# Convolution by three products in place of four from the third double on, both of a double in a row, y carried to its partitions by DMA

## The chip, the cores and the metric

The kernel runs on one core of a Trainium2 chip. The metric is the device time of one execution, in microseconds, and lower is better. The kernel before takes 180.75 us (median of three runs, 180.70 to 180.76).

## The reference, cut to what matters

```
N, C_IN, L = (32, 64, 1024)
C_OUT, K, GROUPS = (64, 9, 4)
out = lax.conv_general_dilated(x, weight, window_strides=(1,), padding=[(4, 4)],
                               dimension_numbers=('NCH', 'OIH', 'NCH'), feature_group_count=GROUPS)
ctx = jnp.einsum('nd,od->no', c, c_weight)
y = out + ctx[:, :, None] + bias[None, :, None]
w = kernel.astype(x.dtype) * 2.0 - 1.0          # 1024 x 1024, signs
x = x + scale * jnp.einsum('bsi,if->bsf', y, w)
```

So each of 32 images (64 channels, 1024 positions) goes through a grouped convolution of nine taps, gets a shift for each channel, and its positions are multiplied by a 1024x1024 matrix of signs; the result, scaled, is added to x. All is float32.

## The kernel before, in words

Two images are a row (128 partitions of x: `2 d + r` is the row, 16 rows), and two rows, r = 0 and 1, are a double d of 0 to 7. `M` = 128, `B` = 8: a position is 8 m + u, and m becomes the partition of y.

**Convolution.** For a row, `to_phases` (L358, ScalarE) splits x into its 8 phases, `x_phase`. SP then issues eight transfers (`to_blocks`, `to_block`, L195) that gather 16 channels x 8 phases into the 128 partitions of a block `x_blk[r][:, a]`; a is one of two images times four groups. `conv` (L650, matmuls at L658) multiplies, for each of the eight blocks, two shifted views of 128 columns (`s` = 0 and 1) with two Toeplitz matrices of the taps, and adds both in PSUM: 16 matmuls a row. `add_shift` (L475, VectorE) adds the shift and writes `y_sum[r]`.

**Products.** y of a double is cut into A11, A12 (row 0) and A21, A22 (row 1). From double 1 on the multiplication by the signs is done in Winograd's form, seven products P1 to P7 in place of eight, with the sums S1 to S4 (`combine`, L492) as operands. Each operand is split in a high part (`high_part`, ScalarE, L373, a cast to fp32r) and a low part (`low_part`, VectorE, L502, the difference), and a product is four matmuls of 512 columns with each (L681). `sum_up` (L513, VectorE) adds a product from its PSUM bank A, B or C to x in `x_nat`; the names of the sums, C11_P2 to C21_A, give the quarter of the output and the bank or product. Double 0 is done with eight plain products (`PLAIN`, L698).

**Order.** Each engine takes its work in the order that is written out in its `step(d)`; semaphores tie the engines together. TensorE in step d: P2, P1, convolution of row 0 of double d + 1, P6, P5, convolution of row 1, P7, P3, P4. ScalarE: the high parts of S3, S4 and A22 of d, the phases of row 0 of d + 2, high parts of A12 and A11 of d + 1, phases of row 1, high parts of S1 and S2 of d + 1. VectorE: the sums as the products end, with the low parts, shifts and combinations between them. SP: the block transfers of both rows of d + 2, the loads of x of d + 3, the stores of d. GpSimd has work in the first 21 us only. `runs(d, 2)` is true where there is a double d + 1, `runs(d, 4)` where there is a d + 2.

## Time and profile before

| what | value |
| --- | --- |
| median of three runs | 180.75 us (180.70 to 180.76) |
| the profiled execution, its own time | 180.59 us |
| its span, first to last instruction | 178.8 us |
| mean granted clock of TensorE | 0.99 |
| TensorE, weight loads, VectorE, ScalarE, GpSimd busy | 171.2, 147.5, 127.5, 68.1, 7.4 us |
| instructions | 2874 |
| DMA | 27.35 MB, 153 GB/s over the span |

Busy is the time in which an engine had an instruction running. The chain of waits follows the work that ended last back to what released it, so it tells which engine sets the time. In the profile an fp32 matmul or weight load is two records. The issue of a transfer is an instruction of its queue; "to landing" is the time from the issue to the last byte.

### The profile page before, as it was taken

To read this page: it belongs to the slowest core of one execution; us is meant where nothing else is said; L and a number is where in the kernel's file an instruction comes from. 1 tells how busy PE (TensorE), PEld (TensorE's weight loads), DVE (VectorE), ACT (ScalarE), POOL (GpSimd) and SP (SyncE) were. 2 spreads that over 40 slices of the span, in tenths; PEclk is the share of its full clock that TensorE was granted. 3 is DMA by queue.
4 is the path that set the end of the run, shared out by engine and by line. 5 is a ranking of instruction groups with operands and counts; after the bars stand their busy time and mean duration, and the time that the engine had idled before them with its cause. 6 is when DMAs were issued, how large, how long until landed. Compare 5 with 4: busy or idle time off the path is not lost.

```text
span 178.8 us, 2874 instructions
## 1 busy us (share of the span) xinstructions
PE 171.2 (96%) x1010; PEld 147.5 (83%) x1010; DVE 127.5 (71%) x188; ACT 68.1 (38%) x77; POOL 7.4 (4%) x18
## 2 busy tenths in 40 slices
PE   7699999999999999999999999999999999998991
PEld 2379888898989889988989898988998898986781
DVE  5736466979996877687675967596766877587662
ACT  3203993566452543329071634237061502042000
POOL 4230600000000000000000000000000000000000
PEclk9969999999999999999999999999999999999999
DMA  5589697768886792776757793778463650005006
GB/s 216 132 152 279 206 262 188 186 105 207 192 283 164 104 343 47 109 167 125 283 84 175 116 318 56 130 146 204 192 96 55 90 233 0 2 0 235 4 0 235
DMA packets 23629, 27.35 MB, mean 153 GB/s; under 512 B 2752, under 2 KB 19072, under 8 KB 23616
## 3 DMA queue, kind: packets, MB, share of 16 engines
q1 hardware_dynamic: 22176, 25.63, 56.8%
q0 software_dynamic: 368, 1.07, 2.4%
q10 hardware_dynamic: 1072, 0.48, 1.3%
q8 instruction: 8, 0.13, 0.3%
q14 instruction: 5, 0.04, 0.1%
HBM read 10.32 MB, written 8.40 MB: 105 GB/s over the span
## 4 chain that ended last, share of the span: by engine, by line
PE 93%; DMA 2%; DVE 1%; ACTq 1%; issue 0%; DVEq 0%
PE ps_conv L658 33%; PE ps_A L681 28%; PE ps_C L681 14%; PE ps_B L681 7%; DMA taps_nat<-weight 2%; PE ps_B L698 2%; PE ps_A L698 2%; PE ps_toep L698 2%; PE ps_C L698 2%; PE ps_toep L681 1%; PE ps_toep L636 1%; PE ps_C L647 1%; DVE sums L214 1%; PE ps_A L624 1%; DVE x_nat L513 0%
## 5 line engine op out<-in xcount | busy, mean ns | idle before, releaser
L658 PEld LDWEIGHTS ps_conv<-toeplitz,x_blk 128*128 128x128 f32 x512 | 60.4, 194 | 2.6 <-issue 0.8
L658 PE MATMUL ps_conv<-toeplitz,x_blk 128*128 128x128 f32 x512 | 60.8, 278 | 0.0
L475 DVE TENSOR_TENSOR y_sum<-ps_conv,shift 128x512 f32<-128x512 f32 (+1 forms) x33 | 22.2, 674 | 17.4 <-PE ps_conv L658 12.4
L373 ACT CAST hi_S<-sums 128x512 fp32r<-128x512 f32 x28 | 16.6, 620 | 43.4 <-DVE sums L492 42.7
L373 ACT CAST hi_A<-y_sum 128x512 fp32r<-128x512 f32 x24 | 14.0, 616 | 41.5 <-DVE y_sum L475 41.5
L358 ACT COPY x_phase<-x_nat 128x1032 f32<-128x1032 f32 x13 | 28.3, 2177 | 3.0 <-DMA x_nat<-x 3.0
L513 DVE SCALAR_TENSOR_TENSOR x_nat<-ps_A,scale_col,x_nat 128x512 f32<-128x512 f32 x27 | 20.3, 750 | 11.2 <-PE ps_A L681 11.2
L502 DVE TENSOR_TENSOR lo_S<-sums,hi_S 128x512 fp32r<-128x512 f32 x28 | 19.0, 680 | 0.0
L502 DVE TENSOR_TENSOR lo_A<-y_sum,hi_A 128x512 fp32r<-128x512 f32 x24 | 16.3, 682 | 1.7 <-ACT hi_A L373 1.7
L681 PE MATMUL ps_A<-sign_T,hi_S 128*128 128x512 f32 x56 | 16.2, 412 | 1.1 <-DVE x_nat L513 0.9
L681 PE MATMUL ps_A<-sign_T,lo_S 128*128 128x512 f32 x56 | 15.0, 389 | 0.0
L513 DVE SCALAR_TENSOR_TENSOR x_nat<-ps_C,scale_col,x_nat 128x512 f32<-128x512 f32 x14 | 10.5, 747 | 3.8 <-PE ps_C L681 3.8
L681 PEld LDWEIGHTS ps_A<-sign_T,lo_S 128*128 128x128 f32 x56 | 10.5, 188 | 2.3
L681 PEld LDWEIGHTS ps_A<-sign_T,hi_S 128*128 128x128 f32 x56 | 9.6, 189 | 2.9 <-issue 1.6
L492 DVE TENSOR_TENSOR sums<-y_sum 128x512 f32<-128x512 f32 x14 | 9.5, 686 | 0.3
L681 PE MATMUL ps_C<-sign_T,hi_S 128*128 128x512 f32 x28 | 7.5, 390 | 0.0
L681 PE MATMUL ps_B<-sign_B,hi_A 128*128 128x512 f32 x28 | 7.5, 389 | 0.0
L681 PE MATMUL ps_B<-sign_B,lo_A 128*128 128x512 f32 x28 | 7.5, 389 | 0.0
L681 PE MATMUL ps_A<-sign_B,hi_A 128*128 128x512 f32 x28 | 7.5, 389 | 0.0
L681 PE MATMUL ps_C<-sign_T,lo_S 128*128 128x512 f32 x28 | 7.5, 389 | 0.0
L681 PE MATMUL ps_C<-sign_B,hi_S 128*128 128x512 f32 x28 | 7.5, 389 | 0.0
L681 PE MATMUL ps_C<-sign_B,lo_S 128*128 128x512 f32 x28 | 7.5, 389 | 0.0
(104 smaller groups left out, 174.3 us busy)
## 6 DMA issues: line engine op xcount, KB each, us to landing
x_nat<-x SPq DMA_DIRECT2D x16, 512.0 KB, 4.2
out<-x_nat SPq DMA_DIRECT2D x15, 512.0 KB, 4.8
x_blk<-x_phase SPq DMA_DIRECT2D x118, 64.5 KB, 2.5
w_bytes<-w_bool SPq DMA_DIRECT2D x2, 512.0 KB, 6.3
shift<-shift_dram POOLq DMA_DIRECT2D x1, 768.0 KB, 6.1
x_blk<-x_phase ACTq DMA_DIRECT2D x6, 64.5 KB, 3.7
x_blk<-x_phase POOLq DMA_DIRECT2D x4, 64.5 KB, 3.0
out<-x_nat SPq DMA_DIRECT2D x1, 256.0 KB, 2.9
```

Source lines behind the costliest of these rows:

```text
L214: return copy(skewed, taps_nat[:, :, :].rearrange("o c k -> o k c").unsqueeze(1) .to_broadcast([C, hi_ - lo_, TAPS, CG]))
L358: nc.scalar.copy(x_phase[r][:, :, 0:M + 1], line(d, r, 0, PAD + L + PAD).rearrange("r (m q) -> r q m", q=B)).then_inc(phase_ok[r], B)
L373: nc.scalar.copy(hi[k][:, :, :], flat(operand(k))).then_inc(hi_ok[k], 1)
L475: nc.vector.tensor_tensor(y_sum[r][:, u, a, :].rearrange("m u a o -> m a u o"), ps_conv[:, a, u, :], shift_of(d, r, a).unsqueeze(2).to_bro ...
L492: nc.vector.tensor_tensor(flat(operand(k)), flat(operand(left)), flat(operand(right)), op).then_inc(s_ok[k], 1)
L502: nc.vector.tensor_tensor(lo[k][:, :, :], flat(operand(k)), hi[k][:, :, :].bitcast(F32), ALU.subtract).then_inc(lo_ok[k], 1)
L513: nc.vector.scalar_tensor_tensor(there, bank[b], scale2_col[:, :], there, ALU.mult, ALU.add).then_inc(summed[k], 1)
L624: nc.tensor.matmul(bank["A"], warm[:, 0:P], warm[:, :], start=True, stop=True)
L636: now = nc.tensor.transpose(ps_toep[:, s, u], taps_exp[:, B * s + u].rearrange("o c q -> o (c q)"), ident[:, :])
L658: now = nc.tensor.matmul(ps_conv[:, a].rearrange("m u o -> m (u o)"), x_blk[r][:, a, s:s + M], toeplitz[:, s, g].rearrange("r u o -> r u ( ...
L681: now = nc.tensor.matmul(dest, part[of][:, u, :], signs[SIGNS_OF[k]][:, KH - 1 - u, c:c + dest.shape[-1]], start=start and u == 0 and part ...
L698: now = nc.tensor.matmul(bank[b], part[of][:, u, :], signs[k][:, KH - 1 - u, :], start=opens and u == 0 and part is hi, stop=not opens and ...
```

## The change

From double 2 on the convolution of a row is made of three products. K = 64: the phase-split positions m are taken as even and odd. Where the four products were even and odd columns with the Toeplitz matrices 0 and 1, now the odd columns are multiplied with the sum of both matrices (`toeplitz[:, 2]`), and the differences of neighbouring columns with one matrix each; the shifted first product is added to the second for even positions, and the third is subtracted for odd ones. A group's two images share a matmul (2 x 64 columns), so there are 3 x 4 matmuls a row.

- GpSimd makes the differences (`differences`), ScalarE copies the odd columns (`odd_blocks`), each for every row.
- VectorE's `fast_y` takes three operations a row and writes `y_two`, whose partitions hold image and half position; ScalarE issues four transfers a row (`to_parity`) that carry it to `y_sum` with the partitions as before.
- Both convolutions stand one after the other, between P1 and P6, and share three PSUM banks.
- Casts and low parts of A11 and A12, of S1 and S2, and of S3 and S4 are made in one instruction each of twice the size (`SPLITS`).
- VectorE makes S3 and S4 after C21_A of the step before; the low part of S12 comes behind C11_P1, that of A behind C22_A.
- On ScalarE the order is S34, odd columns of row 1, A22, both phase copies, the transfers of y, odd columns of row 0 of d + 2, A, S12.
- `x_nat` has 12 slots in place of 16, so the last loads wait for the first stores; each store has a semaphore. The shift is loaded by image in two transfers.

The diff, cut to its core:

```diff
-OPERANDS = "A11", "A12", "A22", "S1", "S2", "S3", "S4"
+OPERANDS = "A11", "A12", "S1", "S2", "S3", "S4", "A22"
+SPLITS = {"A": ("A11", "A12"), "S12": ("S1", "S2"), "S34": ("S3", "S4"), "A22": ("A22",)}
+SPLIT_OF = {k: of for of, ks in SPLITS.items() for k in ks}
...
         x_phase = [sb(f"x_phase{s}", [P, B, PITCH]) for s in range(2)]
-        x_blk = [sb(f"x_blk{s}", [P, NG, PITCH]) for s in range(2)]
-        y_sum = [sb(f"y_sum{r}", [P, B, NG, CG]) for r in range(2)]
-        sums = sb("sums", [P, 4, KH, NG, CG])
+        x_blk = [sb(f"x_blk{s}", [P, NG, BLK_PITCH]) for s in range(2)]
+        y_two = [sb(f"y_two{r}", [P, 2, B, C]) for r in range(2)]
+        y_sum = [sb(f"y_sum{r}", [P, 2, B, C]) for r in range(2)]
+        sums = sb("sums", [P, 4, KH, 2, C])
...
...
+        ps_small = ps_conv[:, 2].rearrange("d g u o -> d (g u o)")
         ps_cond = ps_small[:, 0:N]
         ps_cw = ps_small[:, N:N + C]
...
+        def order(d, r):
+            return 2 * (d - 2) + r
+        def line(d, r, lo_, hi_):
+            return x_nat[:, (2 * d + r) % SLOTS, lo_:hi_]
...
         def to_block(eng, r, a, landed):
-            eng.dma_start(x_blk[r][:, a, 0:M + 1], x_phase[r][a * CG:(a + 1) * CG, :, 0:M + 1]
+            i, g = a // GROUPS, a % GROUPS
+            eng.dma_start(x_blk[r][:, 2 * g + i, 0:M + 1], x_phase[r][a * CG:(a + 1) * CG, :, 0:M + 1]
                           ).then_inc(landed, 16)
...
+        def group(k):
+            if k == "A":
+                return y_sum[0][:, :, :, :].rearrange("m i u c -> m u i c")
+            if k in ("S12", "S34"):
+                n = 0 if k == "S12" else 2
+                return sums[:, n:n + 2].rearrange("m n u i c -> m (n u i c)")
+            return operand(k)
...
         def _(sp):
             def load(d, r, landed):
+                if 2 * d + r >= SLOTS:
+                    sp.wait_ge(stored[2 * d + r - SLOTS], 16)
                 sp.dma_start(line(d, r, PAD, PAD + L), row(x_pairs, d, r)).then_inc(landed, 16)
             def to_blocks(d, r):
-                sp.wait_ge(conv_done[r], 2 * d)
+                if d < 3:
+                    sp.wait_ge(conv_done[r], 2 * d)
+                else:
+                    sp.wait_ge(dif_ok[r], 2 * (d - 2))
+                    sp.wait_ge(odd_ok[r], d - 2)
                 sp.wait_ge(phase_ok[r], B * (d + 1))
                 for a in range(NG):
...
                                   x_nat[:, 2, :].rearrange("r (m q) -> r q m", q=B)).then_inc(phase_ok[0], B)
             pool.wait_ge(shift_out, 16)
-            shift_flat = shift[:, :, :, :].rearrange("p j a o -> p (j a o)")
-            rest = slice(EARLY * C, N * C)
-            pool.dma_start(shift_flat[:, rest], shift_dram[:, rest].to_broadcast([P, N * C - EARLY * C])
-                           ).then_inc(shift_in, 16)
+            for i in range(2):
+                pool.dma_start(shift[i * K:(i + 1) * K].rearrange("p j o -> p (j o)"),
+                               shift_by_image[i:i + 1].rearrange("i j o -> i (j o)").to_broadcast([K, PAIRS * C])
+                               ).then_inc(shift_in, 16)
+            def differences(d, r):
+                if d > 2:
+                    pool.wait_ge(m_done[0], order(d - 1, r) + 1)
+                    pool.wait_ge(m_done[2], order(d - 1, r) + 1)
...
+                for h in range(2):
+                    wait_blocks(pool, d, r, h)
+                for e in range(2):
+                    nc.gpsimd.tensor_tensor(dif[r][:, e], x_blk[r][:, :, e:e + M:2], x_blk[r][:, :, e + 1:e + 1 + M:2][:, :, 0:K],
+                                            ALU.subtract).then_inc(dif_ok[r], 1)
+            for d in range(2, DOUBLES):
+                for r in range(2):
+                    differences(d, r)
...
+            def odd_blocks(d, r):
+                if d > 2:
+                    act.wait_ge(m_done[1], order(d - 1, r) + 1)
+                elif r == 1:
+                    for k in ("B11", "B12", "B21", "B22", "T3"):
+                        act.wait_ge(sign_ok[k], KH)
+                for h in range(2):
+                    wait_blocks(act, d, r, h)
+                nc.scalar.copy(odd[r], x_blk[r][:, :, 1:1 + M:2]).then_inc(odd_ok[r], 1)
+            def to_parity(d, r):
+                act.wait_ge(lo_ok["A" if r == 0 else "A22"], d - 1)
+                for k in (("S2", "S3", "S4") if r == 0 else ("S1", "S3")):
+                    act.wait_ge(s_ok[k], d - 1)
+                for p, made in ((0, y_even_ok), (1, y_odd_ok)):
+                    act.wait_ge(made, order(d, r) + 1)
+                    for i in range(2):
+                        act.dma_start(y_sum[r][p::2, i], y_two[r][i * K:(i + 1) * K, p]).then_inc(y_in[r], 16)
...
             def step(d):
-                for k in ("S3", "S4", "A22"):
-                    high_part(k, d)
+                high_part("S34", d)
+                if runs(d, 2):
+                    odd_blocks(d + 1, 1)
+                high_part("A22", d)
                 if runs(d, 4):
                     to_phases(d + 2, 0)
-                if runs(d, 2):
-                    high_part("A12", d + 1)
-                    high_part("A11", d + 1)
-                if runs(d, 4):
                     to_phases(d + 2, 1)
                 if runs(d, 2):
-                    high_part("S1", d + 1)
-                    high_part("S2", d + 1)
+                    to_parity(d + 1, 0)
+                    to_parity(d + 1, 1)
+                if runs(d, 4):
+                    odd_blocks(d + 2, 0)
+                if runs(d, 2):
+                    high_part("A", d + 1)
+                    high_part("S12", d + 1)
...
+            def fast_y(d, r):
+                n = order(d, r)
+                even, uneven = (y_two[r][:, p].rearrange("m u (g o) -> m g u o", g=GROUPS) for p in range(2))
+                dve.wait_ge(m_done[1], n + 1)
+                dve.wait_ge(shift_in, 32)
+                if d > 2:
+                    dve.wait_ge(y_in[r], 16 * 4 * (d - 2))
+                nc.vector.tensor_tensor(uneven, ps_conv[:, 1],
+                                        shift[:, 2 * d + r].rearrange("m (g o) -> m g o", g=GROUPS).unsqueeze(2)
+                                        .to_broadcast([P, GROUPS, B, CG]), ALU.add).then_inc(mid_ok, 1)
+                dve.wait_ge(mid_ok, n + 1)
+                dve.wait_ge(m_done[0], n + 1)
+                nc.vector.tensor_tensor(even, ps_conv[:, 0], uneven, ALU.add).then_inc(y_even_ok, 1)
+                dve.wait_ge(m_done[2], n + 1)
+                nc.vector.tensor_tensor(uneven, uneven, ps_conv[:, 2], ALU.subtract).then_inc(y_odd_ok, 1)
...
             def step(d):
                 if d > 1:
                     sum_up("C21_A", d - 1)
-                    low_part("S2", d)
+                    combine("S3", d)
+                    combine("S4", d)
                 sum_up("C11_P2", d)
-                low_part("S1", d)
                 sum_up("C11_P1", d)
-                low_part("S3", d)
+                if d > 1:
+                    low_part("S12", d)
                 if runs(d, 2):
-                    add_shift(d + 1, 0, 0)
-                low_part("S4", d)
+                    fast_y(d + 1, 0)
+                low_part("A22", d)
                 if runs(d, 2):
-                    add_shift(d + 1, 0, 1)
-                low_part("A22", d)
+                    fast_y(d + 1, 1)
                 sum_up("C12_A", d)
-                if runs(d, 2):
-                    low_part("A12", d + 1)
+                low_part("S34", d)
                 sum_up("C22_C", d)
-                if runs(d, 2):
-                    low_part("A11", d + 1)
-                    add_shift(d + 1, 1, 0)
-                    add_shift(d + 1, 1, 1)
-                    combine("S1", d + 1)
                 sum_up("C22_A", d)
-                if runs(d, 2):
-                    combine("S3", d + 1)
                 if last(d):
                     finish_last(d)
                 else:
+                    low_part("A", d + 1)
+                    combine("S1", d + 1)
+                    sum_up("C12_C", d)
                     combine("S2", d + 1)
-                    sum_up("C12_C", d)
-                    combine("S4", d + 1)
             first_double()
             for d in range(1, DOUBLES):
...
+            def fast_conv(d, r):
+                n = order(d, r)
+                if n == 0:
+                    pe.wait_ge(y_ok, 16)
+                    pe.wait_ge(both_ok, 1)
+                for m, taps, read in ((1, 2, mid_ok), (0, 0, y_even_ok), (2, 1, y_odd_ok)):
+                    if n:
+                        pe.wait_ge(read, n)
+                    if m == 1:
+                        pe.wait_ge(odd_ok[r], d - 1)
+                    else:
+                        pe.wait_ge(dif_ok[r], 2 * (d - 2) + (1 if m == 0 else 2))
+                    for g in range(GROUPS):
+                        both = slice(2 * g, 2 * g + 2)
+                        of = odd[r][:, both] if m == 1 else dif[r][:, m // 2, both]
+                        now = nc.tensor.matmul(ps_conv[:, m, g].rearrange("m u o -> m (u o)"),
+                                               of.rearrange("r b k -> r (b k)"),
+                                               toeplitz[:, taps, g].rearrange("r u o -> r (u o)"), start=True, stop=True)
+                    now.then_inc(m_done[m], 1)
...
@@ -706,11 +847,10 @@
                 product("P2", d, bank["B"], True, True, "C11_P2")
                 product("P1", d, bank["A"], True, False, "C21_A")
                 if runs(d, 2):
-                    conv(d + 1, 0)
+                    fast_conv(d + 1, 0)
+                    fast_conv(d + 1, 1)
                 product("P6", d, bank["A"], False, False, "C11_P1", 1)
                 product("P5", d, bank["C"], True, False, "C12_C")
-                if runs(d, 2):
-                    conv(d + 1, 1)
                 product("P7", d, bank["A"], False, False, "C12_A", 1)
                 product("P3", d, bank["C"], False, True, "C22_C", 1)
                 if last(d):
```

## Rows read from the trace of the kernel before

**Rows 1.** The page: busy time of the engines; the chain's shares by engine

```profile
PE 171.2 (96%) x1010; PEld 147.5 (83%) x1010; DVE 127.5 (71%) x188; ACT 68.1 (38%) x77; POOL 7.4 (4%) x18
...
PE 93%; DMA 2%; DVE 1%; ACTq 1%; issue 0%; DVEq 0%
```

**Rows 2.** The chain of waits in order of time: start us, us, what

```profile
41.59 1.81 PE ps_B L681 x8
...
65.48 3.57 PE ps_conv L658 x32
...
85.35 3.57 PE ps_conv L658 x32
...
161.19 1.81 PE ps_B L681 x8
...
164.85 0.76 DVE x_nat L513
...
165.75 2.08 PE ps_A L681 x8
```

**Rows 3.** Two steps: busy PE, PEld, DVE, ACT, POOL, granted clock, DMA share, GB/s

```profile
45.20:65.50 20.30, 20.17 (x123) 17.77 (x122) 17.12 (x26) 9.82 (x10) 0.00 (x0) 1.00 0.83 208
65.50:85.35 19.85, 19.85 (x122) 17.64 (x122) 14.60 (x22) 8.24 (x9) 0.00 (x0) 1.00 0.63 135
```

**Rows 4.** Groups by line: the convolution's weight loads; busy us, mean ns

```profile
L658 PEld LDWEIGHTS ps_conv<-toeplitz,x_blk 128*128 128x128 f32 x512 | 60.4, 194 | 2.6 <-issue 0.8 <-DVE toeplitz L219 0.5 <-DMA x_blk<-x_phase 0.4
```

**Rows 5.** Groups by line: VectorE

```profile
L475 DVE TENSOR_TENSOR y_sum<-ps_conv,shift 128x512 f32<-128x512 f32 (+1 forms) x33 | 22.2, 674 | 17.4 <-PE ps_conv L658 12.4 <-issue 4.8
...
L502 DVE TENSOR_TENSOR lo_S<-sums,hi_S 128x512 fp32r<-128x512 f32 x28 | 19.0, 680 | 0.0
...
L447 DVE TENSOR_TENSOR sign_T<-sign_B,sign_T 128x1024 fp32r<-128x1024 f32 x4 | 4.8, 1214 | 0.0
```

**Rows 6.** Groups by line: ScalarE

```profile
L358 ACT COPY x_phase<-x_nat 128x1032 f32<-128x1032 f32 x13 | 28.3, 2177 | 3.0 <-DMA x_nat<-x 3.0
...
L373 ACT CAST hi_S<-sums 128x512 fp32r<-128x512 f32 x28 | 16.6, 620 | 43.4 <-DVE sums L492 42.7
...
L347 ACT ACTIVATE sign_T<-w_bytes 128x2048 fp32r<-128x2048 uint8 x1 | 1.9, 1914 | 0.0
```

**Rows 7.** Instructions in order of time, 85 to 106 us: start us, us, engine

```profile
85.39 0.75 DVE L513 SCALAR_TENSOR_TENSOR x_nat<-ps_A,scale_col,x_nat 128x512 f32<-128x512 f32 x1 [0.47 <-PE ps_A L681]
86.05 0.68 DVE L502 TENSOR_TENSOR lo_S<-sums,hi_S 128x512 fp32r<-128x512 f32 x1
...
88.95 5.05 SPq L195 DMA_DIRECT2D x_blk<-x_phase  x8
...
89.75 1.14 ACT L373 CAST hi_A<-y_sum 128x512 fp32r<-128x512 f32 x2 [5.12 <-DVE y_sum L475]
```

**Rows 8.** Instructions in order of time, 0 to 12 us: block transfers issued

```profile
5.09 5.91 SPq L195 DMA_DIRECT2D x_blk<-x_phase  x6
5.10 2.62 ACTq L195 DMA_DIRECT2D x_blk<-x_phase  x3
...
8.78 2.25 ACTq L195 DMA_DIRECT2D x_blk<-x_phase  x3
```

**Rows 9.** DMA issues: KB each, median us from issue to landing

```profile
x_blk<-x_phase SPq DMA_DIRECT2D x118, 64.5 KB, 2.5
...
out<-x_nat SPq DMA_DIRECT2D x2, 128.0 KB, 2.8
```

**Rows 10.** Instructions in order of time, 12 to 46 us: GpSimd, VectorE, block transfers

```profile
18.45 2.19 POOL L316 COPY x_phase<-x_nat 128x1032 f32<-128x1032 f32 x1 [7.86 <-DMA x_nat<-x]
...
19.53 0.69 DVE L475 TENSOR_TENSOR y_sum<-ps_conv,shift 128x512 f32<-128x512 f32 x1 [1.11 <-PE ps_conv L658]
...
28.32 0.69 DVE L502 TENSOR_TENSOR lo_S<-y_sum,hi_S 128x512 fp32r<-128x512 f32 x1 [3.24 <-ACT hi_S L373]
...
40.11 5.05 SPq L195 DMA_DIRECT2D x_blk<-x_phase  x8
```

222 lines of the change are left out of this document (126 added, 96 removed).

## The prediction

> **What bounds the kernel now.** I read the busy shares first: TensorE 96% of the span, VectorE 71%, ScalarE 38%, GpSimd 4% [rows 1]; in each step the granted clock is 1.00, the upper of its two levels [rows 3]. The chain of waits says the same in order of time: TensorE's work follows on TensorE's work, product by product, 93% of the chain [rows 1, 2]. One step of the pipeline is 19.87 us: seven products of 1.81 us (12.7 us) and two convolutions of 3.57 us (65.48 to 85.35) [rows 2]. In that period VectorE is busy 14.6 us, ScalarE 8.2 us and the DMA engines have a share of 0.6 to 0.8 [rows 3]. The longest gap of TensorE after 50 us is in the last step, where P6 waits for the sum of P1, which ends at 165.61 (P6 starts at 165.75, P1 ended 0.02 before that sum began) [rows 2]. So a shorter convolution is worth its full length, until another engine or a loop of several engines needs more than TensorE does in a step. The question is where that point lies.
>
> **What goes from TensorE.** A convolution of a row is 16 matmuls, 32 records (the trace counts each fp32 matmul twice), in 3.57 us, 0.223 us each [rows 2]. The fast form is 12 matmuls of the same shape, 128x128 weights and 128 moving columns, so 2.68 us. That holds if the weight loads stay hidden: they are as many as the matmuls and 194 ns against a record's pitch of 112 ns looks too long, but the same rows run at that pitch now, overlapped [rows 4]. Without that cover a matmul would cost its two loads, 0.39 us, as the upper bound; 0.223 is the price of the same shapes. Saved: 4 x 0.223 = 0.89 us a row, 1.79 a double; double 2 to 7 have 12 rows, so 10.7 us. TensorE alone would have a step of 18.08 us and the run would come to 180.59 - 10.7 = 169.9 us.
>
> **VectorE in a step.** Removed: four additions of the shift (L475, 0.67 us on the mean, 0.69 for a full one). Added: six operations of 512 elements from PSUM (fast_y), at the price of that same row. The seven low parts become three of 1024 elements and one of 512: 1.21 us for 1024 (L447, f32) against 0.68 for 512 [rows 5], so 4.3 us in place of 4.8. Sums (7 x 0.75 [rows 7]) and combinations (4 x 0.68) stay. Total 4.1 + 4.3 + 5.3 + 2.7 = 16.4 us of records; records overlap by some 0.07 us (one of 0.75 is followed 0.66 later by the next [rows 7]; I take 0.60 for one of 0.68), so about 15 us of 18.08. VectorE isn't the bound by itself. The toeplitz sum, once, 0.7 us, lies in the 3.24 us for which VectorE waits at 28.3 us [rows 10] and costs nothing; if that cover went it would cost 0.7. The low part of S12 moves behind the sum of P1: in the last step it ends 1.2 us after that sum while P6 asks for it 0.9 us after: 0 to 0.3 us.
>
> **ScalarE in a step.** Casts: 0.62 us for 512 elements, the pair at 1.14 [rows 7], so a 1024 one at 1.05 (below: 0.62 plus 512 more at the pace of the 2048-element sign in 1.91 us; above: two single ones, 1.24) [rows 6]. Three and one small: 3.8 us. Two copies of odd columns, 512 elements with a stride: between a cast's 0.62 and half a strided 1032-element copy, 1.09 [rows 6]; I take 0.65, since the stride is 8 bytes and not 32. Two phase copies 2 x 2.18. Eight DMA issues of y at 0.6 to 0.75 [rows 8]: 5 to 6 us. Together some 14.5 us of 18: hidden by size, but not by order, which is the point of the next part.
>
> **The loop that the change closes.** ScalarE takes its work in the order written: hi S34, odd blocks of row 1, hi A22, the two phase copies, the y transfers, then the odd blocks of row 0 of the double after next, and only then hi A of the next double. Those odd blocks need all eight block transfers of a row whose phases were made in this same step. Before, nothing on ScalarE waited for them. And hi S34 waits for S4, which VectorE now makes behind low A, S1, C12_C, S2, C21_A and S3. So, from the end of one S4 to the end of the next:
> hi S34 1.05, odd copy 0.65, hi A22 0.62, phase copy 2.18: 4.5. Eight block issues on SP, the last begins 5.05 - 0.6 = 4.45 after the first, and lands 2.5 later [rows 7, 9]: 6.95. Odd copy 0.65, hi A 1.05: 1.7. On VectorE low A 1.21, S1 0.60, C12_C 0.66, S2 0.60, C21_A 0.66, S3 0.60, S4 0.68: 5.0. Six links between engines at 0.04 (between 0.02 and 0.14 [rows 2]): 0.25. Sum 18.4 us, already above TensorE's 18.08. TensorE feels it where P1 of the next double waits for C21_A, four VectorE operations behind low A, and a stall there holds the whole step.
> To that comes what the y transfers do to the block transfers: they are issued in the same 5 us, by ScalarE while SP issues its eight. Where two and three queues issued at once, at 5 to 11 us, SP took 5.91 us for six (0.98 each) and ScalarE 2.25 for three (0.75) in place of 0.63 [rows 8]; and the y transfers bring 8 x 128 KB more into engines that are 0.6 to 0.8 busy. Their own landing, 2.5 (64.5 KB) to 2.8 us (128 KB) [rows 9], is no term: the last is issued some 10 to 12 us into the step, due at 15.8. Bounds for the slowing of the blocks: nothing (18.4), and 0.35 for each of eight issues (21.2). I take 0.08 each, near the lower end since for most of the time only two queues issue and y's have half the descriptors: **19.1 us a step**.
> The first step has SP's four stores and three loads, DMA share 0.83 [rows 3], and the blocks of row 1 land at 45.2 + 2.0 (issued from 40.11 to 45.16, the last 2.5 after its issue began [rows 9, 10]), after which GpSimd makes two differences before the convolution's second and third part: 0.4 to 0.6 us late, in the same 19.1. The pass after it, which first closes the loop behind those transfers, I put 0.9 higher. Six steps: 6 x 19.1 + 0.9 = 115.5 us, where now 41.59 to 161.19 is 119.6 [rows 2]. The gain is 4.1 us: 180.59 - 4.1 = 176.5, and as the profiled execution is 0.16 under the median of 180.75, **176.6 us**. The other changes are hidden: the store semaphores and 12 slots (the loads of doubles 6 and 7 wait for stores issued in the first step, three steps before), the split shift load, cast and low part of A made as one in the first double (due only at 41.59 [rows 2]); each would cost under 1 us once.
>
> **GpSimd.** It is idle from 21 us on and now gets four differences a step, each of two inputs and 512 elements. Price: the only copy of it is 1032 elements in 2.19 us [rows 10], 2.1 ns an element; so 1.1 us if two inputs cost no more than one, 2.2 if they are read one after the other. Four are 4.4 to 8.8 of 18 us. They are due nearly a step later: hidden, as work. In this trace no VectorE operation with two SBUF inputs runs beside GpSimd: at 19.53 an addition from PSUM took its usual 0.69 within GpSimd's copy [rows 10]; so the price of their meeting lies between nothing (no reason speaks for a gain) and a full stop of one for the length of the other's operation; I take nothing, which is what the one meeting in the rows shows, and keep the other end as the first rival.
> The Trainium skill speaks against the change here: "SBUF — State Buffer", section Who interferes with whom, says that a VectorE instruction with two SBUF inputs and a GpSimd one that reads SBUF exclude each other for their whole length, and that one SBUF input doesn't contend. The 0.69 us addition agrees with the second half; no run here yet shows the first. By it the sum would be the first rival's.
>
> **Rivals.**
> *GpSimd holds VectorE up (slower).* The differences of row 0 start when the blocks land, the same moment as the odd copy; VectorE wants low A 1.7 us later and the two differences last 2.2 to 4.4: a wait of 0.5 to 2.7. Those of row 1 begin some 5 us later, when VectorE makes S3 and S4: half to a whole difference, 0.55 to 2.2. Both lie in the loop. At the low price it is 1.05 a step, 20.15; six make 6.3, so 176.6 + 6.3 - 0.4 (the first pair meets nothing) = 182.5; with differences of 2.2 us it is up to 2.2 + 1.65 more in each step. It turns to slower than before from 0.7 us a step. Against it: VectorE may go first, GpSimd has slack. Low parts and combinations are 7 of VectorE's 16 us, so they do meet.
> *The transfers crowd each other.* y and block packets overlap, and the landing goes from 2.5 to 3.5 us or each issue from 0.63 to 0.8: 18.4 + 1.0 to 1.4 = 19.4 to 19.8 a step, 178.4 to 180.8 (6 x 0.3 to 0.7 above the forecast).
> *TensorE stays the bound.* If the odd copy, the links or the casts are cheaper by 0.4, the loop is below 18.1 and the run 170 to 172. Against it: the sum of 18.4 already has the cheap prices.
> *It doesn't do what it says:* 12 matmuls without accumulation that take as long as 16 would leave 19.87 and add stalls, 181 to 183. The weight loads at the same pitch speak against it.
>
> **How the numbers follow.** Loop near 19.1: 0.41, 173.5 to 179. GpSimd's hold: 0.33, of which 0.07 still under 180.4 (short differences), the rest 181 to 188. Crowded transfers: 0.15, of which 0.07 I count as faster, since the two slowings may add. TensorE the bound: 0.08. The last: 0.03. A measurement of this kernel can tell 0.2%, 0.4 us. Faster 0.41 + 0.07 + 0.07 + 0.08 = 0.63, same 0.05, slower 0.32. The range leaves out TensorE as the bound and the upper part of GpSimd's hold: 173.3 to 184.8; that of the likeliest case alone is 173.5 to 179.
>
> **What the profile of the changed kernel would show.** Convolution rows at 0.223 us a matmul, 144 in place of 192 from double 2 on, and TensorE's other groups as they are; a gap ahead of P1 in each step, released by VectorE (C21_A), of 0.7 to 1.2 us; ScalarE's odd copy released by the block transfers, hi A right behind it; block issues on SP of over 0.63 us while ScalarE issues. Wrong if the gap lies ahead of the convolution's second row (VectorE too slow with fast_y), if low A or S3 on VectorE starts at the end of a GpSimd operation or takes far over 1.2 and 0.68 us (the first rival), or if no gap is there at all.

## The result, and the profile of the changed kernel

The changed kernel takes **190.13 us** (median of four runs, 187.15 to 191.82) where the kernel before takes 180.72 us beside it (180.66 to 180.76): a ratio of **1.042, interval 1.031 to 1.052**. It is slower. The forecast was 176.6 us and the range ended at 184.8. Here and below, a ratio leaves out the executions that took over 1.5% more than the fastest of their kernel (here 190.91 and 191.82 us). The profiled execution took 189.35 us, its span is 187.5 us.

The page of the changed kernel: busy time of the engines, then TensorE's row and the granted clock in 40 slices of 4.69 us.

```profile
PE 168.9 (90%) x914; PEld 140.9 (75%) x914; DVE 139.2 (74%) x180; ACT 71.4 (38%) x68; POOL 37.6 (20%) x43
...
PE   7599999999569999998889969998899978999892
...
PEclk9859999999957999999999999999999999999999
```

TensorE has 96 records less but was 96% of the span and is 90% [rows 1]. There is a hole in the 11th and 12th slice, with a lower clock in the 12th and 13th, and a smaller hole in nearly every step from the third on.

The table goes from the start of P2 to the start of the next P2 on TensorE, by its instructions. ([rows 2] has these starts 0.16 us later, since the chain counts a piece from the end of the one before.) Doubles 1 to 7 give six steps.

| | start to first P2 | 1 | 2 | 3 | 4 | 5 | 6 | last P2 to the end |
| --- | --- | --- | --- | --- | --- | --- | --- | --- |
| before | 41.43 | 20.26 | 19.87 | 19.87 | 19.87 | 19.87 | 19.87 | 17.8 |
| forecast | as before | 19.1 | 20.0 | 19.1 | 19.1 | 19.1 | 19.1 | as before |
| after | 42.95 | 25.05 | 18.55 | 20.85 | 21.01 | 20.17 | 20.72 | 18.2 |

The six steps are 126.35 us where before they were 119.6 (+6.75). With 1.5 us before and 0.4 us behind them that is the 8.7 us by which the span grew. Against the forecast (115.5) they are 10.85 us too long: 5.95 in the first step, 6.35 in the last four, and the second is 1.5 short.

The waits of the changed kernel: who waited for what, us in total, times, the longest.

```profile
ACT set L452 <- DMA x_blk<-x_phase: 27.8, 4, 7.4
...
DVE lo L631 <- ACT hi L483: 7.8, 4, 2.3
...
PE ps_A L822 <- DVE x_nat L642: 6.1, 5, 1.4
...
PE ps_conv L803 <- DVE y_two L595: 5.4, 4, 3.5
```

TensorE waits in two places: ahead of P1 for C21_A (in steps 3 to 6, 1.04 to 1.41 us; the fifth wait is the one in the last step that [rows 2] shows too), which was foretold, and ahead of the second row of the convolution for VectorE's first operation of `fast_y` (3.54 us in the first step, 0.43 to 0.80 in three others), which wasn't. The first line is the loop: ScalarE stands up to 7.4 us at its odd copy for the block transfers. (Odd columns and differences lie in the tile `set_0` for row 0 and in the space of `w_bytes` for row 1, which is why the profile calls them `set` and `w_bytes`.)

**One turn of the loop.** Instructions of the changed kernel in order of time, 84 to 113 us: start us, us, engine, line.

```profile
84.12 2.06 POOL L399 TENSOR_TENSOR set<-x_blk 128x512 f32<-128x512 f32 x2 [14.81 <-DMA x_blk<-x_phase]
...
85.71 1.55 DVE L631 TENSOR_TENSOR lo<-y_sum,hi 128x1024 fp32r<-128x1024 f32 x1 [1.93 <-ACT hi L483]
...
88.70 2.78 POOL L399 TENSOR_TENSOR w_bytes<-x_blk 128x512 f32<-128x512 f32 x2 [2.52 <-DMA x_blk<-x_phase]
...
89.93 1.16 PE L822 MATMUL ps_A<-sign_B,hi 128*128 128x512 f32 x4 [1.35 <-DVE x_nat L642]
90.50 1.54 DVE L621 TENSOR_TENSOR sums<-y_sum,sums 128x512 f32<-128x512 f32 x1
...
94.15 2.09 ACT L440 COPY x_phase<-x_nat 128x1032 f32<-128x1032 f32 x1
...
96.33 6.37 SPq L231 DMA_DIRECT2D x_blk<-x_phase  x8
...
96.62 5.70 ACTq L462 DMA_DIRECT2D y_sum<-y_two  x7
...
105.26 0.67 ACT L452 COPY set<-x_blk 128x512 f32<-128x512 f32 x1 [7.00 <-DMA x_blk<-x_phase]
...
105.83 1.05 ACT L483 CAST hi<-y_sum 128x1024 fp32r<-128x1024 f32 x1
...
106.91 1.55 DVE L631 TENSOR_TENSOR lo<-y_sum,hi 128x1024 fp32r<-128x1024 f32 x1 [2.26 <-ACT hi L483]
```

S4 ends at 92.04; the next one begins at 111.51 and takes 1.52, so the turn is 20.99 us. By the terms of the prediction:

| from S4's end | forecast | after |
| --- | --- | --- |
| hi S34, odd copy, hi A22, phase copy (to 96.24) | 4.5 | 4.20 |
| blocks issued and landed (to 105.26) | 6.95 + 0.64 | 9.02 |
| odd copy, hi A (to 106.91) | 1.7 | 1.65 |
| low A to S4 (to 113.03) | 5.0 | 6.12 |
| links | 0.25 | in the rows above |
| a turn | 19.05 | 20.99 |

The chain of work is the foretold one, link for link; two of its terms are too small.

**The first step.** The same view, 46 to 59 us, and under it the busy time in three stretches (PE, PEld, DVE, ACT, POOL, clock, DMA share, GB/s).

```profile
46.76 2.92 PE L803 MATMUL ps_conv<-toeplitz,set 128*128 128x128 f32 x24
47.85 3.20 DVE L559 TENSOR_TENSOR sign_T<-sign_B,sign_T 128x1024 fp32r<-128x1024 f32 x2
...
48.55 3.40 POOL L399 TENSOR_TENSOR w_bytes<-x_blk 128x512 f32<-128x512 f32 x2 [4.17 <-DMA x_blk<-x_phase]
...
50.97 0.74 DVE L642 SCALAR_TENSOR_TENSOR x_nat<-ps_B,scale_col,x_nat 128x512 f32<-128x512 f32 x1
...
52.48 0.68 DVE L595 TENSOR_TENSOR y_two<-ps_conv,shift 128x512 f32<-128x512 f32 x1
...
53.22 5.49 PE L803 MATMUL ps_conv<-toeplitz,w_bytes 128*128 128x128 f32 x24 [3.54 <-DVE y_two L595]
```

```profile
41.00:66.00 25.00, 21.46 (x107) 18.54 (x106) 19.82 (x23) 9.34 (x9) 7.96 (x6) 0.86 0.85 212
86.00:107.00 21.00, 19.02 (x107) 15.97 (x106) 16.39 (x22) 8.81 (x8) 4.65 (x5) 1.00 0.68 194
51.90:58.80 6.90, 5.58 (x25) 5.59 (x26) 4.59 (x8) 1.76 (x1) 0.05 (x1) 0.51 0.78 185
```

VectorE has the two halves of the sign sums for T4 ahead of C11_P2, C11_P1 and `fast_y`. They start at 47.85 and, beside GpSimd's differences, take 3.20 us where two took 2.4 alone [rows 5]. `fast_y` empties the first bank at 53.16, and only then may the second row start: TensorE has stood for 3.54 us. In that gap the granted clock falls to its lower level, 1.2 GHz (0.51 on the mean from 51.9 to 58.8), and the 24 records take 5.49 us in place of the first row's 2.92.

Rows of the page of the changed kernel: two groups by line (busy us, mean ns) and two kinds of DMA issues (KB each, median us to landing).

```profile
L399 POOL TENSOR_TENSOR set<-x_blk 128x512 f32<-128x512 f32 x12 | 12.8, 1088 | 79.2 <-DMA x_blk<-x_phase 79.2
...
x_blk<-x_phase SPq DMA_DIRECT2D x118, 64.5 KB, 3.2
...
y_sum<-y_two ACTq DMA_DIRECT2D x48, 128.0 KB, 3.3
```

### The profile page after: what moved, and what is told of

It is laid out like the page before. It is cut to its first block and busy times, and to the rows that moved or that the text cites. A ratio compares the mean times of both kernels' runs of the same rounds, so it can differ in the third digit from the quotient of the medians.

```text
span 187.5 us, 2763 instructions
## 1 busy us (share of the span) xinstructions
PE 168.9 (90%) x914; PEld 140.9 (75%) x914; DVE 139.2 (74%) x180; ACT 71.4 (38%) x68; POOL 37.6 (20%) x43
## 5 line engine op out<-in xcount | busy, mean ns | idle before, releaser
L483 ACT CAST hi<-sums 128x1024 fp32r<-128x1024 f32 x14 | 14.7, 1049 | 38.9 <-DVE sums L621 19.8
L399 POOL TENSOR_TENSOR set<-x_blk 128x512 f32<-128x512 f32 x12 | 12.8, 1088 | 79.2 <-DMA x_blk<-x_phase 79.2
L803 PE MATMUL ps_conv<-toeplitz,w_bytes 128*128 128x128 f32 x144 | 20.2, 304 | 5.4 <-DVE y_two L595 5.4
L803 PEld LDWEIGHTS ps_conv<-toeplitz,w_bytes 128*128 128x128 f32 x144 | 19.0, 215 | 6.3 <-DVE y_two L595 6.1
L822 PE MATMUL ps_A<-sign_T,hi 128*128 128x512 f32 x80 | 22.7, 405 | 0.9 <-DVE x_nat L642 0.9
L822 PE MATMUL ps_A<-sign_T,lo 128*128 128x512 f32 x80 | 22.0, 396 | 0.0
L399 POOL TENSOR_TENSOR w_bytes<-x_blk 128x512 f32<-128x512 f32 x12 | 16.8, 1422 | 22.3 <-DMA x_blk<-x_phase 22.3
L803 PEld LDWEIGHTS ps_conv<-toeplitz,set 128*128 128x128 f32 x144 | 16.9, 192 | 0.8 <-issue 0.3
L780 PEld LDWEIGHTS ps_conv<-toeplitz,x_blk 128*128 128x128 f32 x128 | 16.5, 209 | 1.3 <-issue 0.8
L631 DVE TENSOR_TENSOR lo<-sums,hi 128x1024 fp32r<-128x1024 f32 x14 | 17.3, 1238 | 0.0
L803 PE MATMUL ps_conv<-toeplitz,set 128*128 128x128 f32 x144 | 17.1, 275 | 0.0
L780 PE MATMUL ps_conv<-toeplitz,x_blk 128*128 128x128 f32 x128 | 16.7, 294 | 0.0
```

The lines of the kernel that those rows point to most:

```text
L399: nc.gpsimd.tensor_tensor(dif[r][:, e], x_blk[r][:, :, e:e + M:2], x_blk[r][:, :, e + 1:e + 1 + M:2][:, :, 0:K], ALU.subtract).then_inc(di ...
L483: nc.scalar.copy(parts(hi_all, k), group(k)).then_inc(hi_ok[k], 1)
L631: nc.vector.tensor_tensor(parts(lo_all, k), group(k), parts(hi_all, k).bitcast(F32), ALU.subtract).then_inc(lo_ok[k], 1)
L780: now = nc.tensor.matmul(ps_conv[:, i, g].rearrange("m u o -> m (u o)"), x_blk[r][:, 2 * g + i, s:s + M], toeplitz[:, s, g].rearrange("r u ...
L803: now = nc.tensor.matmul(ps_conv[:, m, g].rearrange("m u o -> m (u o)"), of.rearrange("r b k -> r (b k)"), toeplitz[:, taps, g].rearrange( ...
L822: now = nc.tensor.matmul(dest, part[of][:, u, :], signs[SIGNS_OF[k]][:, KH - 1 - u, c:c + dest.shape[-1]], start=start and u == 0 and part ...
```

## The experiments

All ratios are to the kernel before, run beside them on the same chip.

### The loop and the first step: the change again, each of two cures alone, and both

The changed kernel once more, as the partner of the others:

> The changed kernel again, unchanged: the yardstick of this set. It took 187.15 to 191.82 us, and in its profiled execution a step from the third on was 20.2 to 21.0 us, the first 25.05. If the late clock fall in the first step (two stretches at the lower level, about 2.8 us) comes in some executions only, this run should again spread over 2 us and more. A product took 1.86 us there and 1.81 in the kernel before: if that lies in the kernel, it is 1.86 here too; if in the execution, some run shows 1.81.

Measured: 191.85 us, 1.062 (1.057 to 1.067). The steps are 24.39, 19.54, 21.38, 21.45, 21.96 and 21.22; the gap ahead of the second row is 4.12 us in the first step and 0.6 to 1.2 in the others, and the clock falls again. The first P2 starts at 41.72, not at 42.95. The seven executions of this kernel lie between 187.15 and 192.67 us, but the two places are the same.

**ScalarE makes hi A before the odd copy.** This cuts the block transfers out of the loop: hi A then needs only y.

```diff
-                if runs(d, 4):
-                    odd_blocks(d + 2, 0)
                 if runs(d, 2):
                     high_part("A", d + 1)
+                if runs(d, 4):
+                    odd_blocks(d + 2, 0)
+                if runs(d, 2):
                     high_part("S12", d + 1)
```

> ScalarE's copy of the odd columns of row 0 of the double after next is put behind the cast of A, nothing else. Theory of the closed loop (cast, copies, block transfers, copy, cast, low part, four VectorE operations, S3, S4): the cast of A no longer waits for the block transfers, the gap of 1.0 to 1.4 us ahead of P1 goes, and steps 2 to 5 fall from 20.2-21.0 to about 19.2: 6 to 7 us in all, 181 to 183. Rival, VectorE is the bound because GpSimd holds it up: the cast comes earlier but low A, S3 and S4 end as late; under 2 us. Rival, transfers: the y transfers land no earlier than the blocks, the cast of A now waits for them: 2 to 4 us.

Measured: 183.10 us, 1.011 (1.006 to 1.016). Steps 25.03, 18.54, then 19.05, 18.99, 18.89, 18.86. The wait ahead of P1 is gone from the third step on. Instructions of this kernel in order of time, 100 to 104 us:

```profile
100.04 1.05 ACT L483 CAST hi<-y_sum 128x1024 fp32r<-128x1024 f32 x1 [4.24 <-DMA y_sum<-y_two]
...
102.60 1.22 DVE L632 TENSOR_TENSOR lo<-y_sum,hi 128x1024 fp32r<-128x1024 f32 x1
...
103.11 0.67 ACT L452 COPY set<-x_blk 128x512 f32<-128x512 f32 x1 [2.02 <-DMA x_blk<-x_phase]
```

hi A is released by y now, 3 us before the blocks of this row have landed. The gaps ahead of the second row go as well, but for the one in the first step. So the closed loop through the block transfers is the cause of some 1.7 us in each of the last four steps (20.69 to 18.95 on the mean; 2.5 us against the 21.50 of the changed kernel's second execution); the first step doesn't move.

**The sign sums for T4 behind `fast_y`.** The call in the first double becomes a function, called for the low half after `fast_y(2, 0)` and for the high half after `fast_y(2, 1)`.

```diff
-                for u in (LOW, HIGH):
-                    sign_sums("T4", plain("B21", u), ALU.subtract, plain("T2", u), u)
...
                     fast_y(d + 1, 0)
+                if d == 1:
+                    sign_t4(slice(0, KH // 2))
                 low_part("A22", d)
                 if runs(d, 2):
                     fast_y(d + 1, 1)
+                if d == 1:
+                    sign_t4(slice(KH // 2, KH))
```

> In the first step VectorE's two sums for the signs T4 (3.2 us) are put behind the three operations on row 0 of the convolution and behind those on row 1, nothing else. In the profile of the changed kernel TensorE stood 3.54 us ahead of the second row of double 2 for the first of these operations, and the granted clock then fell to the lower level for 6.8 us, in which the row took 5.5 in place of 2.7 us. Theory: the gap of the first step shrinks to under 1 us, the clock stays at the upper level, the step falls from 25.05 to about 19: 187.5 - 6 = 181 to 182. Rival, the differences of row 1 on GpSimd come late anyway (they ended at 51.95): the gap shrinks by 1 us only and the clock still falls.

Measured: 188.49 us, 1.039 (1.032 to 1.046). The first step is 19.88 in place of 25.05; the others are no shorter (21.29, 21.02, 21.59, 20.00, 20.83), so the run gains less than the 6 us that were expected. The same place as above in this kernel:

```profile
48.16 2.05 POOL L399 TENSOR_TENSOR w_bytes<-x_blk 128x512 f32<-128x512 f32 x2 [4.11 <-DMA x_blk<-x_phase]
...
49.76 2.94 PE L808 MATMUL ps_conv<-toeplitz,w_bytes 128*128 128x128 f32 x24 [0.41 <-DVE y_two L595]
...
50.94 1.22 DVE L559 TENSOR_TENSOR sign_T<-sign_B,sign_T 128x1024 fp32r<-128x1024 f32 x1
```

The gap is 0.41 us, the clock stays at its upper level, and the row takes 2.94. The order of VectorE's queue in this one step is shown as the cause of the gap, and the gap as what the fall of the clock hangs on here. The second step gives back up to 2.7 of the 5 us (18.55 to 21.29), which fits with a loop that had time to run ahead while TensorE was late; that reading is argued, not shown.

**Both.**

> Both edits. If the two costs are separate places (the first step, and the loop of steps 2 to 5) they add: 187.5 - 6 - 6.5 = 175 us, under the 180.7 of the kernel before. If VectorE is full as soon as one is mended, less than either sum: 179 and more.

Measured: 179.18 us, 0.989 (0.984 to 0.994); steps 20.04, 20.58, 18.87, 19.65, 19.13, 18.87. Against the changed kernel beside it the first edit gives 4.8%, the second 2.1%, both 6.9% (1.062 to 1.011, 1.039 and 0.989). The two causes are separate and add, and without them the changed form is 1.1% faster than the kernel before. The 175 us that were expected took both gains off the span of the first profiled execution; against the 191.85 us beside it the two give 12.7 us, as forecast (12.5).

### What made the turn of the loop longer than its sum

Both of these stand on the kernel with T4 behind `fast_y`, in which the loop still sets the step and whose own ratio is 1.039.

**GpSimd's differences made small.** From double 3 on, two columns of each block in place of 64, as many instructions as before.

```diff
+                n = K if d == 2 else 2
                 for e in range(2):
-                    nc.gpsimd.tensor_tensor(dif[r][:, e], x_blk[r][:, :, e:e + M:2], x_blk[r][:, :, e + 1:e + 1 + M:2][:, :, 0:K],
-                                            ALU.subtract).then_inc(dif_ok[r], 1)
+                    nc.gpsimd.tensor_tensor(dif[r][:, e, :, 0:n], x_blk[r][:, :, e:e + 2 * n:2],
+                                            x_blk[r][:, :, e + 1:e + 1 + 2 * n:2][:, :, 0:n],
+                                            ALU.subtract).then_inc(dif_ok[r], 1)
```

> On the version with the T4 sums behind the convolution (188.5 us, steps 2 to 5 of 21.3, 21.0, 21.6, 20.0 us), from double 3 on GpSimd's differences take 2 columns of each block in place of 64; the rest of the values is left over from double 2, so the output is not the reference's. It measures what GpSimd's work costs in the loop. If VectorE's two-input operations are stretched by it (in the profile of the changed kernel low A took 1.55 in place of 1.21, S4 1.54 in place of 0.68 beside it), they come back to 1.21 and 0.68, and a step falls by 1.0 to 1.5 us: 182 to 184. If the stretching is harmless because the block transfers set the loop, under 0.4 us a step: over 186.

Measured: 181.65 us, 0.998 (0.994 to 1.003). The same operations of VectorE, first with the full differences (T4 behind `fast_y`), then with small ones:

```profile
86.31 2.50 POOL L399 TENSOR_TENSOR w_bytes<-x_blk 128x512 f32<-128x512 f32 x2 [2.88 <-DMA x_blk<-x_phase]
...
87.82 1.53 DVE L621 TENSOR_TENSOR sums<-y_sum,sums 128x512 f32<-128x512 f32 x1
```

```profile
85.49 0.94 POOL L400 TENSOR_TENSOR w_bytes<-x_blk 128x16 f32<-128x16 f32 x2 [4.67 <-DMA x_blk<-x_phase]
...
86.27 0.71 DVE L623 TENSOR_TENSOR sums<-y_sum,sums 128x512 f32<-128x512 f32 x1
...
91.29 7.71 SPq L231 DMA_DIRECT2D x_blk<-x_phase  x8
...
102.64 1.23 DVE L633 TENSOR_TENSOR lo<-y_sum,hi 128x1024 fp32r<-128x1024 f32 x1 [2.76 <-ACT hi L485]
```

S4 goes from 1.53 to 0.71 us, low A from 1.55 to 1.23, and the stretch from low A's start to S4's end from 6.37 and 6.85 (two turns) to 4.98 and 4.96. That is the forecast's 5.0: the prices of VectorE were right for a GpSimd that is still. In the profiled executions the turns gain less, 0.8 us (mean of steps 2 to 6: 20.94 to 20.14), because the blocks need more: from their first issue to the odd copy 8.6 us became 9.3 (means of four turns), and eight issues took up to 7.71 us. But this profile is of the longest of seven executions (183.12 us) and the one it is held against is of the shortest of three (187.39). By the ratios the edit gives 4.1%, some 7 us, or about 1.4 us for each of the five steps that it reaches.

**The y transfers made small.** Their number and their places in the order stay, each carries 0.5 KB in place of 128.

```diff
-                        act.dma_start(y_sum[r][p::2, i], y_two[r][i * K:(i + 1) * K, p]).then_inc(y_in[r], 16)
+                        act.dma_start(y_sum[r][p::2, i, 0:1, 0:2], y_two[r][i * K:(i + 1) * K, p, 0:1, 0:2]
+                                      ).then_inc(y_in[r], 16)
```

> On the same version, each of the y transfers carries 2 numbers a partition in place of 512; as many are issued, by the same queue. So y is left over from double 1 and the output is not the reference's. It measures what their bytes do to the block transfers, which landed 3.2 us after their issue in place of 2.5 and whose eight issues took 6.4 us in place of 5.05. If the bytes do it, both go back and a step falls by 1.5 to 2 us: 179 to 182. If two queues issuing at once do it, the landing goes back to 2.5 but the issues stay near 6.4 us: 0.7 us a step, 184 to 185.

Measured: 178.91 us (two runs), 0.989 (0.982 to 0.996). That is where the theory of the bytes had put it (179 to 182). From this kernel, its page's DMA issues and then its instructions in order of time:

```profile
x_blk<-x_phase SPq DMA_DIRECT2D x118, 64.5 KB, 2.5
```

```profile
70.05 5.09 SPq L231 DMA_DIRECT2D x_blk<-x_phase  x8
...
89.21 6.14 SPq L231 DMA_DIRECT2D x_blk<-x_phase  x8
...
99.05 1.54 DVE L632 TENSOR_TENSOR lo<-y_sum,hi 128x1024 fp32r<-128x1024 f32 x1 [1.52 <-ACT hi L484]
...
103.64 1.53 DVE L622 TENSOR_TENSOR sums<-y_sum,sums 128x512 f32<-128x512 f32 x1
...
109.46 5.17 SPq L231 DMA_DIRECT2D x_blk<-x_phase  x8
```

The blocks land in 2.5 us again, as before the change [rows 9]; first issue to odd copy is 7.5 us in place of 8.6. Beside ScalarE's small transfers eight issues take 5.09, 6.14, 5.17 and 5.56 us in the last four turns, where with full ones they took 5.62, 5.94, 5.64 and 6.02: mostly they go back towards the 5.05 of the kernel before. The 6.14 is one issue of 1.69 us among seven of 0.6. The kernel before, in which ScalarE issues nothing here, has such ones too: of its nine sets of eight after 50 us, those at 76.30 and 135.89 us took 5.90 and 5.79 us by one issue of 1.4 us each. So it isn't shown that two queues issuing at once lengthen the issues. VectorE's operations are as long as with full transfers (1.54, 1.53): their length isn't the DMA's doing. Steps 2 to 6 are 19.54 on the mean, 1.4 less. The terms of the loop so split: y's bytes 1.1 us (the last of eight blocks lands 2.5 us after its issue in place of 3.4, and is issued 4.9 after the first in place of 5.1), GpSimd 1.1 or more. Of the issues 0.4 is left (4.9, and 4.45 before), whose cause is open.

### Where the products' 5 ns went

In the changed kernel the products take 1.86 us where they took 1.81; the matmuls of 512 columns follow each other at 232 ns in place of 227 (medians of some 380 gaps). For these matmuls only the places of their operands differ. On the kernel with both cures:

```diff
-BLK_PITCH = 130
+BLK_PITCH = 136
...
+        room = sb("room", [P, 32])
         ident = sb("ident", [C, C])
```

With this, the hi and lo tiles (128 columns, the weights) and the signs (512 columns, the moving data) both start at multiples of 256 bytes, as in the kernel before. In the changed kernel hi and lo are 128 bytes off and the signs aren't. Places are worked out from the sizes of the tiles in their order, counted from the first tile.

> On the version with both edits (179.2 us): the block buffers get the pitch of the kernel before (136 in place of 130) and 32 unused numbers stand behind x_nat, so that the high and low parts, the signs and the differences begin at multiples of 256 bytes, as all did before. Theory: the place in SBUF makes a product's matmul 0.2325 us in place of 0.2265; then a product goes back to 1.81 us and 57 of them give 2.8 us: 176.4. Otherwise nothing.

Measured: the pitch is 227 ns. The time wasn't to be told from these two runs, 179.8 and 183.2 us.

The other candidate is the place in PSUM. Here its order is turned round, and the places in SBUF stay as in the changed kernel:

```diff
-        ps_conv = ps("ps_conv", [P, 3, GROUPS, B, CG])
-        bank = {k: ps(f"ps_{k}", [P, BANK])[:, :] for k in ("A", "B", "C")}
         ps_toep = ps("ps_toep", [P, 2, B, C])
+        bank = {k: ps(f"ps_{k}", [P, BANK])[:, :] for k in ("A", "B", "C")}
+        ps_conv = ps("ps_conv", [P, 3, GROUPS, B, CG])
```

> On the same version, the PSUM tiles are laid out so that A, B and C have the banks that they had in the kernel before (the convolution's three come last). Theory: the bank sets the matmul's 0.2325 us; then 1.81 us a product and 176.4. Otherwise nothing: 179.2.

Measured: 232 ns, 180.52 us (two runs, 179.04 and 181.99). The PSUM banks don't matter for it. Then half of the move, `BLK_PITCH = 136` alone: hi and lo start at multiples of 256, the signs 128 off.

> As the version before it, but only the block buffers' pitch is 136: the high and low parts begin at multiples of 256 bytes, the signs (the moving operand) and the differences 128 bytes off. If the weights' place sets the 232 ns of a matmul, it stays at 227 here; if the moving operand's place matters as well, it is 230 or more.

It stays at 232 ns and takes 179.28 us (two runs). And the kernel before with hi and lo moved 128 off and its signs where they were:

```diff
-        x_blk = [sb(f"x_blk{s}", [P, NG, PITCH]) for s in range(2)]
+        x_blk = [sb(f"x_blk{s}", [P, NG, 130]) for s in range(2)]
+        room = sb("room", [P, 32])
```

> The kernel before, with nothing changed but the place of its buffers: block buffers with a pitch of 130 numbers (the columns over 129 were never used) and 32 unused numbers behind x_nat, so that y, the sums and the high and low parts begin 128 bytes behind a multiple of 256, as in the changed kernel, and the signs stay. If the place does it by itself, a product's matmul goes from 227 to 232 ns and the run from 180.8 to 183.6 us (57 products of 0.05 us). If it needs the changed kernel's other traffic, nothing.

The group of the low half of P3 and P4 by line (busy us, mean ns), in turn for the kernel before moved by 128 bytes, for `BLK_PITCH` alone, and for both at multiples of 256:

```profile
L682 PE MATMUL ps_C<-sign_B,lo_S 128*128 128x512 f32 x28 | 7.7, 395 | 0.0
```

```profile
L828 PE MATMUL ps_C<-sign_B,lo 128*128 128x512 f32 x28 | 7.7, 394 | 0.0
```

```profile
L829 PE MATMUL ps_C<-sign_B,lo 128*128 128x512 f32 x28 | 7.5, 389 | 0.0
```

Either one off costs it: 232 ns in both of the first two. In each of the kernels with 232 ns exactly one of the two operands is off; none has both off, so it is open whether each place counts by itself or the difference between them. The kernel before goes to 184.00 us (1.014, 1.012 to 1.017) by that move alone, 2.7 us more than the 181.32 us beside it, where 57 products at 0.05 us were to give 2.8; its step goes from 19.87 to 20.19. So 0.3 us a step come from where tiles happen to lie, which the diff doesn't say in any line. (The two profiled executions differ by 3.6 us, because in the moved one the clock is at its lower level for 6.8 us within the first 15, in place of 3.4. The changed kernel has 6.8 us there in one profiled execution and 3.4 in the other, so that goes with the execution and not with the place.)

### A version that beats both, and what is left in it

Both cures and both places, the kernel of 179.8 and 183.2 us above again, in four more executions:

> The odd columns of row 0 behind the cast of A, the T4 sums behind the convolution, and the buffers moved so that the high and low parts begin at multiples of 256 bytes. With the products at 1.81 us (as the run of that placement showed, 227 ns a matmul) and the steps of the version with both edits (19.5 us on the mean, less 7 x 0.04), it takes 176.5 us, 2% under the kernel before. If VectorE was the bound of those steps, the shorter products only lengthen the gaps: 178.5 to 179.

Measured: **177.78 us, 0.977 (0.970 to 0.983)**, between the two cases of the expectation. That figure rests on three executions; with the two above, the six of this kernel lie between 175.82 and 183.22 us (median 178.8, 1.4% under the kernel before, which took 180.4 to 181.8 beside them). What the places add to both cures can be read from the pitch but not from these times.

The steps are 19.97, 19.26, 19.08, 18.77, 19.59, 19.27. TensorE alone would need some 18.2: seven products at 1.81 and two rows at 2.7 to 2.8. What is left is time lost ahead of P1 and ahead of the second row, 2.6 and 2.9 us over six steps, from start to start. To see whether GpSimd makes it, its differences were put behind S4:

```diff
                     pool.wait_ge(m_done[2], order(d - 1, r) + 1)
+                    pool.wait_ge(s_ok["S4"], d - 1)
```

> The version with all three edits, and GpSimd's differences from double 3 on wait for S4 of the double before, so that they no longer run beside low A, S1, S2, S3 and S4 but beside low S12, A22 and the operations on PSUM. If their meeting is what stretches those from 1.21 to up to 2.04 us and from 0.68 to 1.53, the gaps ahead of P1 go and a step comes to 18.6: 1 to 3 us under the version without the wait. If they only meet low S12 in their place, and with it the first operation on the convolution, nothing is won or a gap ahead of the second row of the convolution grows.

Measured: 178.25 us, 0.977 (0.971 to 0.983), the same. The low parts of the sums by line, first without this wait and then with it:

```profile
L633 DVE TENSOR_TENSOR lo<-sums,hi 128x1024 fp32r<-128x1024 f32 x14 | 17.5, 1251 | 0.0
```

```profile
L634 DVE TENSOR_TENSOR lo<-sums,hi 128x1024 fp32r<-128x1024 f32 x14 | 19.8, 1417 | 0.0
```

The sums became short, and low S12 long in their place (1.64 us at 86.97, beside the differences that start at 85.48). GpSimd's 4.1 us a step meet VectorE's operations with two inputs from SBUF somewhere; the wait only chose which.

The traces show a second thing that holds P1 up in these kernels. S1 needs y of row 1, and where the last of the eight y transfers lands late, VectorE stands ahead of S1. In the kernel with the turned PSUM order:

```profile
97.87 1.23 DVE L632 TENSOR_TENSOR lo<-y_sum,hi 128x1024 fp32r<-128x1024 f32 x1
...
102.57 0.69 DVE L622 TENSOR_TENSOR sums<-y_sum 128x512 f32<-128x512 f32 x1 [3.47 <-DMA y_sum<-y_two]
```

That transfer landed 6.7 us after its issue began, at 102.49, and the step took 22.96 us. In the version of 177.78 us the one large gap ahead of P1 (1.02 us) is of this kind: S1 begins at 118.90, 1.12 late, 0.08 behind a landing that took 5.2 us. With GpSimd's wait it is 1.81 and 1.51 us in the two turns with the largest gaps.

## Why the prediction was wrong

**Right.** TensorE's share: 24 records a row in place of 32, a row needs 2.7 to 2.8 us from its start to the next piece's (2.84 to 2.94 to the end of its last record) against the forecast 2.68 and 3.57 before [rows 2], so the weight loads do stay hidden. The loop from S4 by way of the phase copies, the blocks, the odd copy and hi A back to S4, its order, and the gap ahead of P1 that C21_A releases (1.04 to 1.41 us in four steps, forecast 0.7 to 1.2). ScalarE's prices (odd copy 0.67, casts 1.05), the 1.1 us of a difference (1.03), and the loop as the limit: with its link through the odd copy cut, the step falls to 18.9 to 19.0.

**Term mis-sized: blocks issued and landed.** 6.95 + 0.64 was forecast, 9.02 measured in the turn shown. Over the four last turns the last of eight issues begins 5.3 us after the first (forecast 4.45 + 0.64 = 5.1), so the 0.08 for each was near; the landing was taken as unchanged (2.5), and that of the last block went to 3.4. With y's bytes gone it is 2.5 again. The rival with crowded transfers had the landing at 3.5, and gave 19.4 to 19.8 a step: right in kind, and by itself too small.

**Term mis-sized: VectorE beside GpSimd.** "I take nothing, which is what the one meeting in the rows shows" is the step that failed. That meeting was of an addition from PSUM; low A and S4 read two inputs from SBUF. Low A took 1.55 for 1.21 and S4 1.54 for 0.68, 1.1 us in the turn shown, and small differences took that back (4.98 us for low A to S4). The first rival at its low price, 1.05 a step, is what was seen, and with it the prediction's own sign of it (VectorE's operations taking far over 1.2 and 0.68 us). In time it looks like one operation stopping another: GpSimd's second difference ends at 86.18 and low A, begun at 85.71, ends 1.08 later, at 87.26, 0.13 less than its own length; the pair begun at 88.70 ends at 91.48 and S4, begun at 90.50, ends 0.56 after that. GpSimd pays too, 2.78 us for a pair of 2.06. That one of the two stands for the whole of the other's instruction is what the Trainium skill says in "SBUF — State Buffer", Who interferes with whom; the trace agrees with it to within 0.13 us, where the prediction had set a row on another kind of operands against it.

**Rivals treated as exclusive.** With both mis-sized terms the turn is 19.05 + 1.4 + 1.1 less 0.6 of links and copies, 21.0. The forecast gave each slowing a time with the other at its base price. It said that the two may add, but worked out no time for it; by its own prices 182.5 and another 1.8 to 4.2 us make 184.3 to 186.7, behind the end of its range. They lie one behind the other in the same turn, so they do add.

**Missed: the queue of VectorE in the first step.** The prediction put the first step at 19.1 with 0.4 to 0.6 us of lateness inside, and asked only when the blocks land. It didn't list what stands ahead of `fast_y` on VectorE: two sign sums of 1.2 us each, which wait for nothing there and had no reader before P4 of the same step. The gap was 3.54 us, GpSimd stretched the two sums by 0.8, and the clock that fell in the gap made the row 2.6 us longer. The step is 5.95 us over the forecast, nearly half of the miss; 5.2 of them go with the order of the queue (25.05 to 19.88). The prediction named a gap ahead of the convolution's second row as a sign that VectorE is too slow with `fast_y`: the gap came, but in the first step from the order and not from the load, for moving the two sums closes it to 0.41. The smaller ones in later steps (0.43 to 0.80, and up to 1.26 with the sign sums moved) go when the loop is cut.

**Missed: the price of a product.** "TensorE's other groups as they are" was wrong by 0.05 us a product: 0.35 a step, 2.1 us in six, and about 0.4 us each ahead of them and behind. In the changed kernel the loop hides part of it. The start, forecast as unchanged, was 1.5 us late, of which the pitch is about 0.4. The other 1.1 go with the execution: in the kernel's second profiled one the start is 0.3 late (41.72).

**Second step.** It was put 0.9 above the others and came out 1.5 below that. With the first step mended it is 21.29. That fits with a loop that was ahead because TensorE came late from the first step; this is argued, not shown.

**Sum.** Start 1.5, first step 5.95, second -1.5, the four others 6.35, the end 0.4: 12.8 us (rounded), the difference of the span (187.5) to the forecast's (174.7). The median is 0.8 us above the profiled execution, which makes 13.5 us of 176.6 to 190.13.

## What to carry to other kernels

A wait put into an in-order queue makes a loop of everything behind it: write the turn down by its links, and price every link under the load that the same change adds, with the slowings added and not as alternatives. For the one step in which the new form begins, list each engine's queue ahead of the first new operation; work that nobody needs yet belongs behind it. And before a small gain is read off TensorE, compare the pitch of the same matmuls in both traces: where buffers came to lie took 1.4% here.
